# One sum of 512 elements behind both products, in place of a sum of 256 for each half, in the recurrence of a hybrid transformer block

## What is computed

```python
def step(S, xs):
    r_t, w_t, k_t, v_t, a_t, b_t = xs
    sa = jnp.einsum('bhij,bhj->bhi', S, a_t)
    S = S * jnp.exp(w_t)[:, :, None, :] + sa[..., None] * b_t[:, :, None, :] + v_t[..., None] * k_t[:, :, None, :]
    o_t = jnp.einsum('bhij,bhj->bhi', S, r_t)
    return (S, o_t)
```

## Time and profile before

| what | us |
|---|---|
| median of three runs | 4290.1 (4286.33 to 4292.08) |
| the profiled execution, its own time | 4289.99 |
| its span, first to last instruction | 4288.3 |
| TensorE busy | 3784.4 (88%) |
| VectorE busy | 3104.9 (72%) |
| ScalarE busy | 2315.4 (54%) |
| GpSimd busy | 2109.1 (49%) |
| VectorE's first and last product of the recurrence | 2225.3 and 3757.2 |

### The profile page before, as it was taken

How to read it: one execution, slowest core, us unless ns; L and a number is a source line. 1 busy time by engine, 2 the same in 40 slices (tenths; PEclk the granted TensorE clock), 3 DMA queues, 4 the chain that set the end, 5 groups by cost and what they waited for, 6 DMA issues and landing times. The chain is left out here.

```text
span 4288.3 us, 68819 instructions
## 1 busy us (share of the span) xinstructions
PE 3784.4 (88%) x22244; PEld 2628.1 (61%) x22244; DVE 3104.9 (72%) x8038; ACT 2315.4 (54%) x7477; POOL 2109.1 (49%) x1867
## 2 busy tenths in 40 slices
PE   5999999999996599699959999999999999957698
PEld 2344444444443556466637888888888888856465
DVE  5778777777773511288859999999999999957210
ACT  1666666666665411266633666666666666623211
POOL 2212212212211522133339999999999999903322
PEclk7999999999998599899979999999999999977699
DMA  4323323323353533155452323332333333167242
GB/s 112 81 75 82 87 71 82 90 73 77 82 116 91 168 106 121 45 191 192 182 151 31 43 37 42 38 41 39 40 39 40 40 39 41 22 183 257 64 135 79
DMA packets 466722, 377.92 MB, mean 88 GB/s; under 512 B 298860, under 2 KB 424585, under 8 KB 460228
## 3 DMA queue, kind: packets, MB, share of 16 engines
q1 hardware_dynamic: 454084, 348.38, 33.4%
q0 software_dynamic: 12288, 25.28, 1.7%
HBM read 221.61 MB, written 159.58 MB: 89 GB/s over the span
## 5 line engine op out<-in xcount | busy, mean ns | idle before, releaser
L750 DVE TENSOR_REDUCE at_neg_max<-at_slot 128x1 f32<-128x512 f32 (+3 forms) x1216 | 745.9, 655 | 247.9 <-PE at_slot L542 245.1
L672 ACT ACTIVATE at_prob<-at_slot 128x512 f32<-128x512 f32 (+1 forms) x1216 | 631.1, 577 | 354.5 <-PE at_slot L562 353.7
L390 POOL TENSOR_SCALAR_AFFINE_SELECT at_prob<-at_prob 128x512 f32<-128x512 f32 x256 | 162.8, 636 | 887.6 <-ACT at_prob L672 887.4
L2082 ACT ACTIVATE sc_seen<-sc_state 128x512 f32<-128x512 f32 x256 | 270.4, 1056 | 543.5 <-DVE sc_prod L2025 538.8
L2191 PE MATMUL sc_ps_o<-sc_terms,sc_ident 128*128 128x256 f32 x2048 | 535.0, 380 | 1.5 <-DVE sc_o_buf L1999 1.5
L2025 DVE TENSOR_TENSOR sc_prod<-sc_state,sc_three 128x384 f32<-128x384 f32 x1024 | 519.2, 549 | 3.7 <-POOL sc_from_v L1901 3.7
L1929 POOL TENSOR_TENSOR sc_terms<-sc_seen,sc_pack 128x1024 f32<-128x1024 f32 (+2 forms) x288 | 491.5, 1740 | 0.0
L542 PE MATMUL at_slot<-at_k_stack,at_q_stack 96*128 96x512 bf16 (+3 forms) x1536 | 458.1, 334 | 24.7 <-DMA at_k_stack<-parts 22.3
L1907 POOL TENSOR_TENSOR sc_outer<-sc_pack 128x2048 f32<-128x2048 f32 x128 | 470.2, 3674 | 5.0
L2169 PE MATMUL sc_added<-sc_outer,sc_ident 128*128 128x128 f32 x3072 | 429.1, 276 | 48.5 <-POOL sc_outer L1914 43.5
L2169 PEld LDWEIGHTS sc_added<-sc_outer,sc_ident 128*128 128x128 f32 x3072 | 417.6, 192 | 83.8 <-issue 45.1
(11 more groups left out here) (310 smaller groups left out, 7025.6 us busy)
## 6 DMA issues: line engine op xcount, KB each, us to landing
packed<-pr_pack SPq DMA_DIRECT2D x16, 3072.0 KB
sc_pack<-packed SPq DMA_DIRECT2D x512, 96.0 KB, 3.7
parts<-at_parts SPq DMA_DIRECT2D x96, 256.0 KB
f_up_w<-in_ffn_wi SPq DMA_DIRECT2D x16, 1024.0 KB
f_down_w<-in_ffn_wo SPq DMA_DIRECT2D x16, 1024.0 KB
at_q_stack<-parts SPq DMA_DIRECT2D x32, 384.0 KB
at_k_stack<-parts SPq DMA_DIRECT2D x32, 384.0 KB
slots<-at_no_row SPq DMA_DIRECT2D x2, 4128.0 KB
```

Of the source, the lines that this page charges most:

```text
L672: act.activation(prob[:, first:first + n, q1 - tiles * P:q1], ps[:, 0:n * tiles * P].rearrange("p (n k) -> p n k", n=n), ACT.Exp)\
L750: dve.tensor_reduce(neg_max[:, chunk, qt, h:h + n], ps[:, 0:n * tiles * P].rearrange("p (n k) -> p n k", n=n), AX.X, ALU.max, negate=True) ...
```

## The change

The two sums of a pair become one operation of 512 elements into 32, over both halves. It stands behind both products and waits for the second of them (`base + 2`); its output goes to the same places in `u`, with the halves' rows interleaved by the access pattern. Both rank products of the first step stand behind one wait, for that sum (`base + 3`), in place of a wait for each half. As there is one operation less to a pair, `OPS` becomes 8, and the numbers that name a later operation go down by one: the state writes' wait, and TensorE's wait for the rank products. ScalarE's wait is written with `OPS` and names the same products.

```diff
-        OPS = 9
+        OPS = 8
...
+                    dve.wait_ge(chain, base + 2)
+                    dve.tensor_reduce(u[:, pair, :, :].rearrange("p s (h i) -> p h s i", h=2),
+                                      prod[:, :, 0:2].rearrange("p h s (i j) -> p h s i j", j=D),
+                                      AX.X, ALU.add).then_inc(chain, 1)
+                    dve.wait_ge(chain, base + 3)
                     for h in range(2):
-                        dve.wait_ge(chain, base + 1 + h)
-                        dve.tensor_reduce(u[:, pair, :, rows[h]],
-                                          prod[:, h, 0:2].rearrange("p s (i j) -> p s i j", j=D),
-                                          AX.X, ALU.add).then_inc(chain, 1)
-                    for h in range(2):
-                        dve.wait_ge(chain, base + 3 + h)
                         dve.tensor_tensor(rank[:, 0, part_of[h]].rearrange("p (i j) -> p i j", j=D),
...
-                    dve.wait_ge(chain, base + 7)
+                    dve.wait_ge(chain, base + 6)
...
-                    pe.wait_ge(chain, CHAIN + 1 + (g * PAIRS + n) * OPS + 5 + h)
+                    pe.wait_ge(chain, CHAIN + 1 + (g * PAIRS + n) * OPS + 4 + h)
```

## The result

The changed kernel takes 4392.55 us (4392.28 to 4393.46, 4 runs) against 4291.09 for the kernel before beside it: a ratio of 1.0242 on record, with an interval of 1.0229 to 1.0254 (the two medians alone give 1.0236). It is slower by 101.5 us; 97 were forecast.

What follows compares the result with a forecast made beforehand. VectorE's own order in the recurrence was taken as the bound: 0.04 + 0.68 + 0.04 = 0.76 us in place of 0.57, 0.19 more in each of 512 pairs; 4290.0 + 97.3 = 4387.3 us, range 4365 to 4425.

Steps and rivals of the forecast that it cites:

- The bound: In the recurrence, the chain runs through VectorE's own order; TensorE is on it only from first rank product to state write.
- The two waits: Ahead of the sum and the first rank product: a gap of 0.04 us each, 0.12 a link from start to start.
- The few rows of the late normalisation: Behind the recurrence: operations start 0.46 us apart when waiting for the one ahead, 0.34 when not.
- The gap behind a PSUM write: Between the sum and the first rank product: taken as 0.04 us; rival 0.24, 102 us more, 4490 us, chance 4%.
- the far end of 0.24: Upper case for the gap behind the sum's PSUM write: 0.24 us, 102 us more, 4490 us, chance 4%.
- the memset of the earlier trace: Memset that waits for the very last state write and starts 0.24 us after that write's end.
- The sum: The one sum of 512 elements in place of two: 0.68 us, with bounds of 0.666 and 0.836.
- The two runs of the input: Rival at the sum: two-run input costs as two operations do, 0.836 us; 80 us more, 4467 us, chance 3%.
- The range: Whole kernel: 0.15 to 0.25 us a pair gives 4367 to 4418 us; range set at 4365 to 4425.
- Nothing is hidden: Behind the first rank product, no late TensorE work covers the added 0.19 us a pair; rival all hidden, 4290 us, 2%.
- The row that the prediction leaned on for this: Start of the recurrence: TensorE busy 15.35 of 20 us, 77%, at clock 1.00; against the clock-loss rival, chance 1%.
- The rival on the other side: At the sum and first rank product, the overlap survives: path 0.50 us for 0.57, 36 us less, 4254 us, chance 6%.

Runs made afterwards that it cites:

- the filled link: Changed kernel with a memset of one element a partition, read by nothing, between the sum and the first rank product: 4390.57 us, ratio 1.0238.
- the fastest kernel: Kernel before with the second half's sum and second step's rank product split, so no operation waits for the one directly ahead: 4274.74 us, ratio 0.9965.

## Why the prediction was right

Point by point, by its own steps:

- *The bound.* The chain was VectorE's own order with TensorE hanging on it. TensorE's added wait, 105.0 us, is about the growth of the stage, 104.5 us.
- *The two waits.* Forecast 0.12 us from start to start for each. Alone they measure 0.127 and 0.138, in which the linked operation's own 0.01 us more is included; the gaps are 0.034 each, at 0.04 forecast. The few rows of the late normalisation, behind the loop, were enough to price 1024 links.
- *The gap behind a PSUM write.* Taken as 0.04 against the far end of 0.24. It is 0.034. What holds the memset of the earlier trace rows back 0.24 was not tested; it stays open. Part of it may be the memset's own, since the one in the filled link starts late without waiting for anything.
- *The sum.* The step that was mis-sized, by little: 0.68 taken, 0.695 measured, 0.015 x 512 = 8 us. Two small parts were missing, the write into PSUM (9 ns) and the longer reading of a linked operation (12 ns). The two runs of the input, which I had feared, cost nothing. Two more small errors went opposite ways. The gaps at 0.034 in place of 0.04 take 6 us off for 1024 of them. The first rank product, now linked, reads about 10 ns longer, and the second one starts 0.208 us behind it in the mean in place of 0.198; the prediction had this at nothing, and it adds 5 us. 97 + 8 - 6 + 5 = 104, and the stage grew by 104.5. That the forecast is within 5 us of the result is in part due to errors that cancel. Of the whole kernel's growth, 101.5 us by the medians, the interval of the ratio reaches from 98 to 109 us.
- *The range.* It was added up slightly too narrow. Its own unknowns (gaps of 0.034 to 0.06, the sum at 0.666 to 0.70, 0.02 of reading error) make 0.14 to 0.27 us a pair, 74 to 138 us, where 0.15 to 0.25 was taken; the upper end would be 4428, above the 4425 stated. The measured 0.204 us lies well inside either.
- *Nothing is hidden.* The growth of a plain pair was forecast at 3.11 - 2.92 = 0.19; it is 3012.02 - 3008.89 = 3.13, so 0.21. The gap ahead of the state write moved along and absorbed nothing, as argued: VectorE's idle time there, most of it in gaps too short to be listed among the waits of the earlier trace rows, is the same before and after:

```profile
L2060 DVE TENSOR_TENSOR sc_state<-sc_added,sc_rank 128x128 f32<-128x128 f32 x1024 | 254.5, 294 | 50.7 <-PE sc_added L2180 16.4
```

```profile
L2059 DVE TENSOR_TENSOR sc_state<-sc_added,sc_rank 128x128 f32<-128x128 f32 x1024 | 254.6, 294 | 50.8 <-PE sc_added L2179 14.0
```

ScalarE and GpSimd only wait longer. The clock stayed at 1.00 at a busy share of 89%. The row that the prediction leaned on for this, 20 us at 77% and a clock of 1.00, was weak evidence: with u in SBUF TensorE is busy the same 77%, over 400 us, and the granted clock there is 0.91.
- *The rival on the other side*, that the overlap survives and 36 us are gained, needed waits on the neighbour that cost nothing. The merging by itself does gain: from both waits without it (138 us) to the change (101.5 us) it is some 36 us, 0.07 us for one operation saved. The change bought it with two links of 0.13.

## What to carry to other kernels

On a VectorE chain that bounds the kernel, count for each operation whether it needs the result of the one directly ahead: such a link cost 0.13 us here, an operation saved gave 0.07. So two short operations that alternate with others, each needing the result of the one before last, beat one long operation between two links here; merge only where no new link comes in. And the idle column shows only a quarter of a link (0.034 us); to see the rest, compare start to start.

## What the runs showed of the hardware that was not expected

A VectorE product with both inputs in SBUF took 660 ns in the mean where the same with one input in PSUM took 281, because it waited for the GpSimd operation under way; moving 1 KB a partition from PSUM to SBUF cost 675 us. Whoever moves a small operand between the memories has to look at what GpSimd does at that moment.

Where VectorE has no gap left, in the fastest kernel, its operations read 9 to 19 ns longer in the mean (the product of 384 elements 560 ns in place of 549), though start to start they are no slower. Why is open.
